# The last context tile is projected to keys and values at full width

## The reference, cut to what matters

```
K = key @ Wk.T + bk      # (16, 1601, 256), 16 heads of 16
V = value @ Wv.T + bv
qk = Q K^T               # per head
scores = qk / 4          # its mean, mean of row maxima and mean row variance of
                         # its softmax go through a small MLP that gives t per head
attn = softmax(qk / (2 t))
out = attn V, then @ Wo.T + bo
```

## Time and profile before

| | before |
|---|---|
| median of three runs | 1201.48 us |
| the profiled execution | 1205.8 us |
| its span, first to last instruction | 1203.9 us |
| mean granted TensorE clock | 0.918 of full speed |
| TensorE busy (matmuls) | 1121.5 us, 93% |
| VectorE busy | 812.9 us, 68% |
| ScalarE busy | 763.1 us, 63% |
| GpSimd busy | 405.0 us, 34% |

### The profile page before, as it was taken

One profiled execution on the slowest core, in us unless ns is written; L12 is line 12 of the kernel. 1 busy time (PEld: TensorE's weight loads), 2 busy tenths in 40 slices (PEclk: granted clock), 3 DMA queues, 4 the chain that ended last, 5 costly groups with the idle time before them and its releaser, 6 DMA issues.

```text
span 1203.9 us, 39710 instructions
## 1 busy us (share of the span) xinstructions
PE 1121.5 (93%) x15215; PEld 914.4 (76%) x15215; DVE 812.9 (68%) x2128; ACT 763.1 (63%) x1547; POOL 405.0 (34%) x420
## 2 busy tenths in 40 slices
PE   3868799999999999999999999999999999999965
PEld 2545588888888787878887887878888888877743
DVE  4466667677776776677767777586767777766255
ACT  2434477776756676677766776767776777665521
POOL 2267352223232331443143333243234324310223
PEclk9957799898979998999989998999899999988777
DMA  4611010201010111101020101101010200000000
GB/s 133 195 29 27 14 37 12 62 11 43 18 40 25 37 30 28 37 4 53 11 54 12 46 20 37 29 17 48 24 33 12 55 11 20 4 5 3 7 1 9
DMA packets 46817, 38.93 MB, mean 32 GB/s; under 512 B 14576, under 2 KB 46000, under 8 KB 46640
## 3 DMA queue, kind: packets, MB, share of 16 engines
q1 hardware_dynamic: 46640, 36.41, 11.0%
HBM read 34.30 MB, written 2.10 MB: 30 GB/s over the span
## 4 chain that ended last, share of the span: by engine, by line
PE 82%; DVE 9%; issue 3%; ACT 2%; DMA 2%; POOL 1%; SPq 1%; DVEq 0%; ACTq 0%; POOLq 0%
PE s1p L716 15%; PE s2p L747 13%; PE pjp L662 13%; PE pjp L669 13%; PE pvp L764 10%; PE s2p L679 3%; PE tlp L860 2%; PE tlp L854 1%; DVE est L1407 1%; PE tlp L799 1%; PE tlp L878 1%; PE s2p L737 1%; DVE negm L1401 1%; PE s2p L649 1%; PE tlp L821 1%
## 5 line engine op out<-in xcount | busy, mean ns | idle before, releaser
L1401 DVE TENSOR_REDUCE negm<-s1p 128x1 f32<-128x400 f32 (+1 forms) x512 | 289.9, 566 | 181.6 <-PE s1p L716 179.2
L1060 ACT ACTIVATE ering<-s1p,negm 128x400 f32<-128x400 f32 (+1 forms) x512 | 303.8, 597 | 117.4 <-DVE negm L1401 112.2
L1071 ACT ACTIVATE pring<-s2p 128x512 f32<-128x512 f32 x427 | 241.4, 567 | 145.9 <-PE s2p L747 142.6
L1407 DVE BATCH_NORM_STATS2 est<-ering 128x6 f32<-128x400 f32 (+1 forms) x512 | 290.7, 568 | 19.9 <-ACT ering L1060 19.9
L716 PE MATMUL s1p<-kt,qbd 32*128 32x400 f32 (+1 forms) x1024 | 292.3, 585 | 10.6 <-ACT ering L1060 8.2
L747 PE MATMUL s2p<-q2bd,kt 32*128 32x128 f32 (+1 forms) x3192 | 237.9, 279 | 0.0
L747 PEld LDWEIGHTS s2p<-q2bd,kt 32*128 32x128 f32 (+1 forms) x3192 | 226.9, 191 | 6.3
L662 PE MATMUL pjp<-cr,wkv 128*128 128x256 f32 (+1 forms) x1344 | 197.4, 300 | 27.5 <-DVE vt L1373 19.4
L662 PEld LDWEIGHTS pjp<-cr,wkv 128*128 128x128 f32 x1344 | 176.3, 203 | 44.0 <-issue 27.7
L1279 POOL TENSOR_TENSOR cr<-stage,cr 128x512 fp32r<-128x512 f32 (+1 forms) x112 | 130.4, 1165 | 217.8 <-ACT cr L1051 217.8
L669 PE MATMUL pjp<-wkv,cr 128*128 128x256 f32 (+1 forms) x1200 | 181.0, 301 | 7.8 <-ACT kt L1033 7.8
(11 more groups left out here) (280 smaller groups left out, 1110.7 us busy)
## 6 DMA issues: line engine op xcount, KB each, us to landing
stage<-in_ctx SPq DMA_DIRECT2D x96, 256.0 KB, 2.9
qbd<-q_dram SPq DMA_DIRECT2D x128, 8.0 KB, 1.6
stage<-in_ctx SPq DMA_DIRECT2D x16, 65.0 KB, 2.6
vt<-in_x SPq DMA_DIRECT2D x1, 1024.0 KB, 6.7
q_dram<-late SPq DMA_DIRECT2D x1, 1024.0 KB, 4.7
late<-in_x SPq DMA_DIRECT2D x7, 128.0 KB, 2.2
out_y<-late SPq DMA_DIRECT2D x7, 128.0 KB, 1.7
late<-in_gate SPq DMA_DIRECT2D x1, 768.0 KB, 5.0
```

Of the source, the lines that this page charges most:

```text
L1060: nc.scalar.activation(ering[:, u % 3, 0:w], s1p[u % 3][:, 0:w], ACT.Exp, bias=negm[s.par][:, p, c:c + 1]).then_inc(s1_exp, 1)
L1071: nc.scalar.activation(ring_place(s, v)[0:m, 0:n], s2_bank(s, v)[0:m, 0:n], ACT.Exp).then_inc(s2_exp, 1)
L1401: nc.vector.tensor_reduce(negm[s.par][:, p, ch:ch + 1], s1p[u % 3][:, 0:w], AX.X, ALU.max, negate=True).then_inc(s1_max, 1)
L1407: nc.vector.bn_stats(est[:, p, ch, :], ering[:, u % 3, 0:CH[ch][1]]).then_inc(s1_sum, 1)
```

## The change

Three places in `project` change. The key group of the last tile streams all 256 columns of the slot, where it streamed 66. The value group of the last tile takes all 128 columns of the slot's first block as its stationary operand and writes all 128 partitions of the bank, where it took and wrote 65. The number of matmuls, their order, the waits and all other engines' code stay.

```diff
                 if what[0] == "k":
-                    n = 2 * P if w < VU - 1 else KEVEN
                     for g in range(DB):
                         for cp, wp, d in parts:
-                            mm = nc.tensor.matmul(bank[:, 2 * P * g:2 * P * g + n], wkv[:, 0, wp, d, P * g:P * g + P],
-                                                  c[:, cp, d, 0:n], start=(cp + wp + d == 0),
+                            mm = nc.tensor.matmul(bank[:, 2 * P * g:2 * P * g + 2 * P], wkv[:, 0, wp, d, P * g:P * g + P],
+                                                  c[:, cp, d, :], start=(cp + wp + d == 0),
                                                   stop=((cp, d) == (1, 1)))
                 else:
                     for j in range(min(2, KTILES - 2 * w)):
-                        m = P if 2 * w + j < KTILES - 1 else KLAST
                         for cp, wp, d in parts:
-                            mm = nc.tensor.matmul(bank[0:m, D * j:D * j + D], c[:, cp, d, P * j:P * j + m],
+                            mm = nc.tensor.matmul(bank[:, D * j:D * j + D], c[:, cp, d, P * j:P * j + P],
                                                   wkv[:, 1, wp, d, :], start=(cp + wp + d == 0),
                                                   stop=((cp, d) == (1, 1)))
```

## The result

The changed kernel takes 1185.8 us (median of four runs, 1181.39 to 1188.68). The kernel before, run beside it, takes 1202.56 us (four runs, 1199.61 to 1203.65). The ratio on record is 0.9854 (the medians alone give 0.9861), with a 95% interval of 0.9822 to 0.9886: faster by 1.5%. The forecast was 1187 us, with a range of 1179 to 1199. The profiled execution took 1186.36 us with a span of 1184.4, against 1205.8 and 1203.9 before. Three runs further down, two of the nineteen of the kernel before beside k_only and one of the eight of extra190, ran at a lower granted clock than their like; they count in the medians given there, but not in the ratios.

A forecast was written before the change was run, and what follows sets the result against it. TensorE, busy for 93% of the span, was taken as the bound. Clock falls gone (19.1 us) less direct costs (1.9 and 0.9) gave 16.3 us less: 1189.5 us from the profiled execution, 1185.2 from the median, middle 1187, range 1179 to 1199.

The forecast's parts named there:

- The falls go: Granted clock no longer falls behind the last tile's key group once widened: 19.1 us less together; chance 0.67.
- The value of 65.6 and 63.3 us for a stretch: Sign: key group to key group, elements 4 to 14, second and first kind of slot, at clock 1.00.
- Direct cost of the key group: Last tile's key group on TensorE: 256 columns instead of 66 cost 0.12 us per element, 1.9 us in all.
- Direct cost of the value group: Last tile's value group on TensorE: one longer load shows, 0.055 us per element, 0.9 us in all.
- The sum: Whole kernel: 19.1 us from the clock less direct costs of 1.9 and 0.9, 16.3 us less.
- 15.9 + 1.06: Clock falls gone: 15.9 us for five in the second kind of slot, 1.06 us for element 13's.
- element 2: One fall behind its key group, some 3.4 us at half clock, expected to go: 1.1 us less.
- two starting points: Gain taken from the profiled execution's 1205.8 us gives 1189.5, from the median 1201.48 gives 1185.2; the middle was forecast.
- the clock does not heed the width: Rival: falls behind the key group stay, only direct costs of 2.8 us remain, 1204.3 us; chance 0.11.
- the falls move into the work behind the group: Rival: three of five falls reappear in later scores and value products, 9.5 us come back, 1196.5 us; chance 0.13.
- More falls than before: Rival: elements 0.18 us longer, so those that escaped also get falls, 7.4 us more, 1211.7 us; chance 0.09.

The follow-up runs named there:

- k_only: Against the kernel before, only the last tile's key group widened to 256 columns, value group left narrow: 1183.89 us, ratio 0.9854.
- extra190: Kernel before, its 66-column key group kept, plus twelve matmuls of 190 columns whose result nobody reads: 1208.38 us, ratio 1.0037.
- k130: Against the kernel before, the last tile's key group widened to 130 columns, value group left narrow: 1188.47 us, ratio 0.9867.
- v_only: Against the kernel before, only the last tile's value group widened to 128 stationary columns, key group left at 66: 1203.85 us, ratio 0.9990.
- extra66: Kernel before, its 66-column key group kept, plus twelve matmuls of 66 columns whose result nobody reads: 1242.78 us, ratio 1.0335.
- narrow14: Kernel before, with two further 66-column matmuls in the last tile's key group whose result nobody reads: 1205.60 us, ratio 1.0026.
- wide_second: Against the kernel before, the last tile's key group widened to 256 columns in even elements only, value group narrow: 1186.81 us, ratio 0.9875.

## Why the prediction was right

**The falls go: shown.** No fall behind the key group in elements 4 to 15, in the changed kernel, k_only and k130; six in v_only. The value of 65.6 and 63.3 us for a stretch is met by 65.59 to 65.76 and 63.23 to 63.28, but for element 8's with its stray fall.

**Direct cost of the key group.** Forecast 0.12 us per element. In timelines it is 0.10 us in element 8, 1.56 against 1.46. Element 14, the only one of the second kind that had the full clock before, has grown from 65.46 to 65.63 us with both groups, where 0.12 + 0.055 was forecast. The first kind has grown less than that, from 63.17 to 63.23 to 63.28 us. So both groups together cost about 2 us in 16 elements by these stretches (an estimate), where 2.8 was forecast.

**Direct cost of the value group.** Forecast 0.055 us, measured 0.04 to 0.05: 0.81 us in v_only and 0.82 us after, against 0.77. The rule by which each of the six loads would show (the Trainium skill, TensorE: Matmul & The Clock Gate, the section on packing small matmuls) would make it 0.33 us by the 55 ns of the earlier trace rows; the measurement decides against it here. The prediction let one load show, the first of the group, and the trace bears that out. The second to sixth matmuls of the same two groups, narrow before and wide in v_only:

```profile
671.70 0.76 PE L669 MATMUL pjp<-wkv,cr 128*65 128x256 f32 x5
...
669.13 0.75 PE L669 MATMUL pjp<-wkv,cr 128*128 128x256 f32 x5
```

From the first matmul to the second it is 0.17 us before (671.53 to 671.70) and 0.23 us in v_only (668.90 to 669.13); from the second to the next group it is 0.60 and 0.58 us. So the longer load shows once, and the other five not at all. That the loads did grow is seen in the least load of the values' line; it is now 186 ns, after 133:

```profile
L668 PEld LDWEIGHTS pjp<-wkv,cr x1200: 186/188/337, 49.4 to 1047.0; 128*128 128x128 f32 x172
```

**The sum.** Forecast 16.3 us; medians give 16.8, profiled executions 19.4. The forecast of 1187 us lies 1.2 us from the median. By pieces of the profile the terms were not all of the right size. The eleven stretches gained 12.2 us, where 15.0 follow from the terms (15.9 + 1.06, less eleven direct costs); the stray fall in element 8's stretch took 2.9 of that back. Up to element 4's key group 5.4 us were gained (335.18 became 329.79), where 0.4 was forecast (1.1 less four direct costs). Behind element 15's key group 1.9 us were gained, where 0.9 follows from the terms. The term mis-sized is element 2. Its stretch at a clock of 0.95 was 62.81 us,

```profile
207.85:270.66 62.81, 62.25 (x932) 52.77 (x925) 41.39 (x102) 46.30 (x93) 16.04 (x16) 0.95 0.13 36
```

and is 60.21 now. Besides the fall of the earlier trace rows it had a second, 12.7 us behind the key group, which the prediction did not count:

```profile
217.40:220.40 3.00, 2.44 (x52) 1.69 (x49) 2.97 (x8) 2.22 (x6) 0.41 (x1) 1.00 0.00 0
220.60:223.80 3.20, 3.20 (x16) 3.13 (x16) 1.18 (x3) 1.98 (x5) 1.56 (x2) 0.50 0.16 23
```

Both are gone after the change, so 2.6 us came from there and not 1.1. Why the second went is not shown; with 130 columns the first went and a later one came. Elements 0 and 3 gave 1.8 and 1.2 us more, for which the sum had no term, only the range; they have falls in other places in the profiles, and why those differ was not tried.

So the falls behind the key group went as forecast, at a direct cost a little below the forecast. That the time came out within 1.2 us is in part luck: the gain in the first elements was 5 us larger than forecast, and a stray fall took 2.9 us back. The 1187 was also the middle between two starting points 4.3 us apart, and single runs of the kernel before differ by more than that.

**The rivals.** That the clock does not heed the width is refuted by k_only and by the pair extra190 and extra66. That the falls move into the work behind the group happened in no profile. Stray falls stood elsewhere: one after the change and two in k130, in the next slot's MLP, and one in extra190. Unlike the seven before, each of the four had a gap of 0.3 to 0.6 us in TensorE's work shortly before it. The 5 us before the one after the change:

```profile
640.40:645.40 5.00, 4.68 (x42) 3.47 (x30) 4.79 (x14) 2.77 (x5) 1.47 (x2) 1.00 0.00 0
```

Element 2's second fall had one, too (2.44 of 3.00 us busy, above). What brings the stray falls was not tried. More falls than before did not come with the change. The reason that this rival gave, a longer way alone, does not hold: narrow14 has seven falls and extra190 none, with groups longer by two matmuls and by twelve. The escapes do end in extra66, where the group streams few columns for longer; it takes 38 us more, of which 21.5 were expected as direct cost. The busy time of TensorE could not have told these apart. The rule in the Trainium skill (the same page, the section on why this matters for your kernels) that names gaps between bursts does not account for the falls behind the key group: TensorE was busy for 7.80 of 7.80 us before element 8's, and the trace shows no gap in the 8 us before any of the other six.

**Which version is best.** Four kernels, the changed one, k_only, k130 and wide_second, have ratios of 0.9854, 0.9854, 0.9867 and 0.9875 with intervals that overlap. None beats the changed one beyond doubt.

## What to carry to other kernels

A row of busy time that is full says nothing about the clock: read the granted clock in stretches with the same work, and where it falls, look at the group just before. Two stretches with the same instructions, one with a fall and one without, give the price. A matmul that streams few columns behind a stationary operand of 128 could be widened almost for nothing here, 0.1 us for twelve, and that was worth far more than the columns that it was meant to save. A control with as many matmuls of few columns tells whether it was the width.

## What was not expected of the hardware

The pace of the key group's matmuls hardly depends on their width: 1.46 us for twelve of 66 columns, 1.56 to 1.58 us of 256 at full clock, and between them 1.48 us of 130 in element 8 of k130:

```profile
593.06 1.56 PE L662 MATMUL pjp<-cr,wkv 128*128 128x130 f32 x12
594.54 0.94 PE L716 MATMUL s1p<-kt,qbd 32*128 32x400 f32 x4
```

And the twelve further matmuls per element add 3.6 us to the median with 190 columns each, hardly clear of nothing (0.9999 to 1.0075), since the falls go with them, but 38 us with 66.
